# First cross attention of a gated Flamingo block: one half of the heads' softmax moves from VectorE to ScalarE, head by head

## The chip, the core and the metric

The kernel runs on one core of one Trainium2 chip. The metric is the device time of one execution in microseconds (us); the median of three executions of the kernel before is 763.54 us, from 762.81 to 764.01. The engines are named as in the profile: PE is the matmul engine (TensorE; PEld is its weight load), DVE is VectorE, ACT is ScalarE, POOL is GpSimd, SP issues transfers. A row that begins with L451 belongs to line 451 of the kernel before.

## What is computed

Two gated layers stand in a row, each a cross attention and a feed-forward part. The change touches the first cross attention alone:

```python
q = (query @ Wq + bq).reshape(B, SQ, H, HD).transpose(0, 2, 1, 3)       # H = 16 heads, HD = 8
k = (key_value @ Wk + bk).reshape(B, SK, H, HD).transpose(0, 2, 1, 3)   # SK = 77 keys
scores = jnp.einsum('bhqd,bhkd->bhqk', q, k) * scale                    # scale = 8 ** -0.5
scores = jnp.where(key_padding_mask[:, None, None, :], -jnp.inf, scores)
attn = jax.nn.softmax(scores, axis=-1)
attn_out = jnp.einsum('bhqk,bhkd->bhqd', attn, v) ...
attn_out = attn_out @ Wo + bo
```

There are 4 batches of 512 queries, so 16 tiles of 128 queries. For one tile the scores are 16 x 77 = 1232 numbers on each of 128 partitions.

## The kernel before

The program is written out by hand, stage by stage, engine by engine: each engine runs its instructions in the order of its block, and named semaphores hold it where it needs another's result. There is no scheduler. The stage in question runs from about 43 to 147 us of the span and takes one tile `n` in each turn of a loop; the 16 heads are two halves, `h` = 0 and 1, of 616 columns each. PSUM banks 0 and 1 hold the scores of half 0, banks 2 and 3 those of half 1, and there is one copy of each.

What is done for a tile, in the order of its data:

- PE, `score(n, h)` (lines 497 to 508): two small matmuls with the mask (L502) and two with the scores (L506). It may overwrite the banks when `s_used` says that the half of tile n-1 has been read.
- DVE, `top(n, h)` (L444): the maximum of each head. `shifted(n, h)` (L451): the scores less the maximum, from PSUM into the tile `sh` in SBUF; this counts up `s_used`.
- ACT (L570): the exponential of `sh`, one instruction for eight heads, into `pr` (the profile calls it xy, since it lies in that tile). It counts up `exp_done`.
- DVE, `total(m, h)` (L458): the sum of each head's exponentials, into `den`; `inverse(m, h)` (L465): its reciprocal `rd`.
- POOL (L589): probabilities times `rd`; this counts up `pn_done`. Up to tile 9 POOL does a further instruction of preparation for later stages behind each tile.
- PE, `flip(m, b)` (L517): ten transposes of the probabilities in three groups (4, 4 and 2), for the tile two turns back (m = n-2). ACT copies the result from PSUM into `pt` (L560, the first eight; L562, the last two).
- PE (L546): ten products with the values, each as two passes; ACT copies the result with a bias into `attt` (L576); PE projects it one turn later (L531), and DVE adds it to `base` (L474).

The order on each engine in one turn n of the loop: PE runs flip(n-2, 0), the projection of n-3, flip(n-2, 1), flip(n-2, 2), score(n+1, 0), the products of n-2, score(n+1, 1). ACT runs the two copies for n-2, the exponentials of both halves of n, `attt` of n-2. DVE runs top and shifted of (n, 0), the addition of n-3, total(n-1, 0), top(n, 1), inverse(n-1, 0), shifted(n, 1), total(n-1, 1), inverse(n-1, 1).

Of the kernel before, what the change touches and what calls it, by code (L numbers as in the profile page):

```python
# [12 lines left out]
ALU = mybir.AluOpType  # L13
# [3 lines left out]
P = 128  # L17
# [83 lines left out]
def flamingo_kernel(nc, a, out):  # L101
    with ExitStack() as ctx:
        def sb(name, shape, dt=F32, scope=ctx):
            return scope.enter_context(nc.sbuf_tensor(name, shape, dt))
# [70 lines left out]
        @contextmanager  # L175
        def stage(*names):

            with ExitStack() as c:
                sems = [c.enter_context(nc.semaphore(n)) for n in names]
                with nc.Block() as block:  # L180
                    yield block, sems
                nums = [s.num for s in sems]
                nc.all_engine_barrier(sems_to_clear=range(min(nums), max(nums) + 1))
# [44 lines left out]
        with ExitStack() as early:  # L228
# [187 lines left out]


            with ExitStack() as scope:
                sh = sb("sh", [P, 2, WA], scope=scope)
                pr = xy[:, 0:3 * CA * P].rearrange("p (i c) -> p i c", i=3)  # L420
                pt = sb("pt", [P, 2, CA, P], scope=scope)
                qf = [sb(f"qf{i}k", [P, D], scope=scope) for i in range(3)]
                LS, LP, LO = 1, 2, 3

                with stage("v_chain", "d_chain", "p_chain", "pads_done", "s_raw", "s_used", "exp_done", "rd_done", "pn_done",
                           "pt_raw", "pt_lo", "pt_hi", "a_raw", "a_done", "r_raw", "r_done") as (block, sems):
                    (v_chain, d_chain, p_chain, pads_done, s_raw, s_used, exp_done, rd_done, pn_done,
                     pt_raw, pt_lo, pt_hi, a_raw, a_done, r_raw, r_done) = sems
                    WH, HH = WA // 2, HA // 2

                    def scores(h):
                        return banks(2 * h, 2).rearrange("p (b c) -> p b c", c=512)[:, :, 0:G4].rearrange(
                            "p b (h k) -> p b h k", k=SK)
# [4 lines left out]
                    @block.vector  # L438
                    def _(dve):
                        v, d = Chain(dve, v_chain), Chain(dve, d_chain)  # L440

                        def top(n, h):
                            dve.wait_ge(s_raw, 4 * n + 2 * h + 2)
                            v.do(dve.tensor_reduce(mx[:, n % 2, HH * h:HH * (h + 1)].rearrange("p (b h) -> p b h", b=2),  # L444
                                                   scores(h), AX.X, ALU.max))

                        def shifted(n, h):
                            if n >= 2:
                                dve.wait_ge(exp_done, 2 * (n - 2) + h + 1)
                            v.sync()  # L450
                            dve.tensor_tensor(  # L451
                                sh[:, n % 2, WH * h:WH * (h + 1)].rearrange("p (b h k) -> p b h k", b=2, k=SK), scores(h),
                                mx[:, n % 2, HH * h:HH * (h + 1)].rearrange("p (b h) -> p b h", b=2).unsqueeze(3).broadcast_to(
                                    [P, 2, 4, SK]), ALU.subtract).then_inc(s_used, 1)

                        def total(m, h):
                            dve.wait_ge(exp_done, 2 * m + h + 1)
                            d.do(dve.tensor_reduce(den[:, m % 2, HH * h:HH * (h + 1)], probs(m, h), AX.X, ALU.add))  # L458

                        def inverse(m, h):  # L460
                            if m >= 2:
                                dve.wait_ge(pn_done, 2 * (m - 2) + h + 1)
                            d.sync()
                            c = slice(HH * h, HH * (h + 1))
                            dve.reciprocal(rd[:, m % 2, c], den[:, m % 2, c]).then_inc(rd_done, 1)  # L465

                        for n in range(NT + LO):
                            if n < NT:
                                top(n, 0)
                                shifted(n, 0)  # L470
                            if n >= LO:
                                m = n - LO
                                dve.wait_ge(r_raw, m + 1)
                                dve.tensor_tensor(base[:, m, :], bank[7][:, 3 * P:4 * P], base[:, m, :], ALU.add).then_inc(r_done, 1)  # L474
                            if LS <= n < NT + LS:
                                total(n - LS, 0)
                            if n < NT:
                                top(n, 1)
                            if LS <= n < NT + LS:
                                inverse(n - LS, 0)  # L480
                            if n < NT:
                                shifted(n, 1)
                            if LS <= n < NT + LS:
                                total(n - LS, 1)
                                inverse(n - LS, 1)
                            if n == NT:
                                dve.wait_ge(late_in, LATE_IN)
                                v.do(dve.tensor_tensor(sprod[:], fscale[:, 0:1], fscale[:, 1:2], ALU.mult))
                                v.do(dve.reciprocal(rscale[:], fscale))
                                v.sync()  # L490
                                v.do(dve.tensor_scalar(qf[0][:], kern[:], rscale[:, 1:2], None, ALU.mult))
                                v.sync()
                                quantise(dve, v, qf, kern_q[:], D)

                    @block.tensor
                    def _(pe):
                        def score(n, h):
                            u, j = divmod(n, TPB)
                            if n:
                                pe.wait_ge(s_used, 2 * (n - 1) + h + 1)  # L500
                            for g in (2 * h, 2 * h + 1):
                                pe.matmul(bank[g][:, 0:G4], ones_bf[32 * g:32 * g + 1, :],  # L502
                                          mrow_bf[32 * g:32 * g + 1, u:u + 1, :].broadcast_to([1, 4, SK]), start=True, stop=False)
                            for g in (2 * h, 2 * h + 1):
                                rows_g = slice(32 * g, 32 * g + 32)
                                pe.matmul(bank[g][:, 0:G4], qt[rows_g, u, j * P:(j + 1) * P],  # L506
                                          kbd_a[rows_g, u, 4 * g:4 * g + 4, :].rearrange("p h k -> p (h k)"), start=False,
                                          stop=True).then_inc(s_raw, 1)
# [43 lines left out]
                    @block.scalar  # L552
                    def _(act):
                        for n in range(NT + LP):
                            if n >= LP:
                                m = n - LP
                                if m >= 2:
                                    act.wait_ge(a_raw, m - 1)
                                act.wait_ge(pt_raw, 3 * m + 2)
                                act.activation(pt[:, m % 2, 0:8, :].rearrange("p c q -> p (c q)"), banks(4, 2), ACT.Copy).then_inc(pt_lo, 1)  # L560
                                act.wait_ge(pt_raw, 3 * m + 3)
                                act.activation(pt[:, m % 2, 8:10, :].rearrange("p c q -> p (c q)"), bank[6][:, 0:2 * P],  # L562
                                               ACT.Copy).then_inc(pt_hi, 1)
                            if n < NT:
                                for h in range(2):
                                    act.wait_ge(s_used, 2 * n + h + 1)
                                    if n >= 3 and h == 0:
                                        act.wait_ge(pt_raw, 3 * (n - 2))
                                    c = slice(WH * h, WH * (h + 1))
                                    act.activation(pr[:, n % 3, c], sh[:, n % 2, c], ACT.Exp, scale=DA ** -0.5).then_inc(exp_done, 1)  # L570
                            if n >= LP:
                                m = n - LP
                                act.wait_ge(a_raw, m + 1)
                                if m >= 2:
                                    act.wait_ge(r_raw, m - 1)
                                act.activation(attt[:, m % 2, :], bank[7][:, 0:P], ACT.Identity,  # L576
                                               bias=cols_a[:, 2:3]).then_inc(a_done, 1)
# [1093 lines left out]
```

## Time and profile before

| | us |
|---|---|
| median of three executions | 763.54 |
| the profiled execution, its own time | 767.54 |
| its span, first to last instruction | 765.8 |
| of it the stage that changes | about 43 to 147 |
| busy PE / DVE / POOL / ACT, whole span | 592.9 / 503.5 / 418.2 / 345.0 |

The profiled execution is 4.0 us longer than the median of those without a profile. The busy shares above are means over about ten stages with different limits; only this stage bears on the change, and it is read from the engine timelines and the waits of that stretch. In the timeline a row gives the start in us, the duration, engine, line, operation, what it writes and reads, and in brackets the idle time ahead of it with what ended that.

### The profile page before, as it was taken

What the parts mean: (1) busy time and instruction counts of PE and PEld (TensorE: products, weight loads), DVE (VectorE), ACT (ScalarE), POOL (GpSimd) and SP (SyncE); (2) the same over time, 40 slices, a digit from 0 to 9 for tenths busy, and PEclk for the clock granted to TensorE, in tenths of its full rate; (3) what the DMA queues carried; (4) which work ended last, traced back from release to release, by engine and by line L of the source; (5) the groups of instructions that cost most, each with busy time, mean ns of one, the idle gap of its engine ahead of it and who ended that gap; (6) DMA issues with size and microseconds to landing.
All of it is one profiled execution on the core that took longest, in us unless ns stands there. A gap on an engine that the chain in (4) does not pass through costs nothing. (4 is left out here: it accounts for less than half of the span.)

```text
span 765.8 us, 13331 instructions
## 1 busy us (share of the span) xinstructions
PE 592.9 (77%) x4922; PEld 419.2 (55%) x4922; DVE 503.5 (66%) x1117; ACT 345.0 (45%) x603; POOL 418.2 (55%) x345
## 2 busy tenths in 40 slices
PE   5679999595287999997598799999867945768701
PEld 3337777564244677776355367777753623555500
DVE  2766888636558888874543788888636336676496
ACT  2334545271156656654443566566516223343221
POOL 4545673362269999980401999999404015554320
PEclk9558999988689999999899999999998967788755
DMA  8500000000011111110000111111000000000001
GB/s 267 152 1 2 1 1 1 1 1 0 1 28 37 36 30 30 43 23 1 2 1 0 43 35 38 30 30 43 10 1 1 0 1 0 1 0 1 0 1 55
DMA packets 16142, 18.16 MB, mean 24 GB/s; under 512 B 4261, under 2 KB 10831, under 8 KB 16079
## 3 DMA queue, kind: packets, MB, share of 16 engines
q1 hardware_dynamic: 14639, 14.70, 7.5%
q10 hardware_dynamic: 1440, 2.61, 1.0%
q8 instruction: 40, 0.66, 0.4%
q14 instruction: 23, 0.19, 0.1%
HBM read 8.01 MB, written 1.05 MB: 12 GB/s over the span
## 5 line engine op out<-in xcount | busy, mean ns | idle before, releaser
L209 POOL TENSOR_TENSOR rstd<-rstd,minus_half 128x4 f32<-128x4 f32 x32 | 34.0, 1062 | 145.1 <-DVE rstd L203 145.1
L1102 POOL TENSOR_TENSOR rn<-n,minus_half 128x16 f32<-128x16 f32 x32 | 93.7, 2929 | 2.7
L1098 POOL TENSOR_TENSOR qk<-qk 128x512 f32<-128x512 f32 x64 | 80.1, 1273 | 10.8 <-DVE qk L1033 10.8
L1030 DVE TENSOR_TENSOR qk<-ps,rt 128x512 f32<-128x512 f32 x64 | 44.0, 688 | 49.1 <-ACT sq L985 33.4
L1004 ACT ACTIVATE ptb<-ps 128x512 f32<-128x512 f32 x64 | 34.7, 595 | 73.6 <-PE ps L858 73.6
L1107 POOL TENSOR_TENSOR qk<-qk,rn 128x512 f32<-128x512 f32 x64 | 65.4, 1043 | 2.5
L589 POOL TENSOR_TENSOR xy<-xy,rd 128x616 f32<-128x616 f32 x32 | 38.9, 1216 | 42.3 <-DVE rd L465 42.3
L985 ACT ACTIVATE sq<-ps 128x512 f32<-128x512 f32 x64 | 37.6, 598 | 21.9 <-PE ps L821 8.1
L546 PE MATMUL ps<-pt,vbd_a 128*128 128x128 f32 x320 | 41.7, 288 | 6.5 <-ACT pt L560 6.5
L546 PEld LDWEIGHTS ps<-pt,vbd_a 128*128 128x128 f32 x320 | 39.0, 200 | 13.5 <-issue 12.6
L1366 POOL TENSOR_TENSOR sh_c<-gt_c,mx 128x616 f32<-128x616 f32 x16 | 19.9, 1242 | 45.5 <-DVE mx L1328 45.5
L828 PEld LDWEIGHTS ps<-consts,qk 128*128 128x128 f32 x256 | 29.2, 140 | 27.4 <-issue 15.6
L1033 DVE TENSOR_TENSOR qk<-ps,rt 128x512 f32<-128x512 f32 x64 | 43.6, 681 | 0.0
L1240 DVE SCALAR_TENSOR_TENSOR qk<-ps,cols_b,pb 128x512 f32<-128x512 f32 (+1 forms) x24 | 17.8, 749 | 37.6 <-PE ps L1137 27.7
L1067 DVE TENSOR_REDUCE mx<-ps 128x8 f32<-128x1024 f32 x32 | 39.0, 1218 | 4.4 <-PE ps L852 4.4
L828 PE MATMUL ps<-consts,qk 128*128 128x128 f32 x256 | 35.3, 276 | 7.8 <-POOL qk L1107 5.4
L1071 DVE TENSOR_TENSOR pb<-ps,mx 128x1024 f32<-128x1024 f32 x32 | 39.2, 1225 | 3.0
L865 PE MATMUL ps<-vv,ptb 128*64 128x65 f32 x512 | 36.5, 224 | 4.6 <-DVE xy L1056 4.6
L893 PE MATMUL ps<-wo_b,ont 128*128 128x128 f32 x256 | 34.6, 278 | 7.0 <-ACT ont L1011 7.0
L1060 DVE TENSOR_REDUCE n<-sq 128x16 f32<-128x1024 f32 x32 | 38.7, 1209 | 0.0
L978 ACT ACTIVATE qkt<-ps 128x512 f32<-128x512 f32 x64 | 35.5, 598 | 6.8 <-PE ps L828 6.8
L850 PE MATMUL ps<-qkt 64*64 64x128 f32 x512 | 36.0, 280 | 2.8 <-ACT qkt L978 2.8
(200 smaller groups left out, 1634.6 us busy)
## 6 DMA issues: line engine op xcount, KB each, us to landing
vv<-vv SPq DMA_DIRECT2D x62, 130.0 KB, 2.3
wqkv<-in_wqkv SPq DMA_DIRECT2D x1, 1536.0 KB, 16.5
x<-in_x SPq DMA_DIRECT2D x4, 256.0 KB, 8.7
out<-xy SPq DMA_DIRECT2D x4, 256.0 KB, 2.3
w_b<-in_w_b SPq DMA_DIRECT2D x1, 682.0 KB
tmat<-in_tmat SPq DMA_DIRECT2D x1, 616.0 KB, 7.7
w<-in_w ACTq DMA_DIRECT2D x1, 512.0 KB, 4.1
rot<-in_c_rot ACTq DMA_DIRECT2D x1, 512.0 KB, 8.3
```

The costliest lines, as they stand in the source:

```text
L546: mm = pe.matmul(bank[7][:, 0:P], vbd_a[:, c, m // TPB, :], pt[:, m % 2, c, :], start=(c == 0), stop=(c == CA - 1))
L589: pool.tensor_tensor(probs(m, h), probs(m, h), rd[:, m % 2, HH * h:HH * (h + 1)].unsqueeze(2).broadcast_to([P, HH, SK]), ALU.mult).then_in ...
L828: t = pe.transpose(dst[:, c * P:(c + 1) * P], qk[:, m % 3, kind, c * P:(c + 1) * P], ident)
L985: act.activation(sq[:, kind, :], src, ACT.Square).then_inc(done, 1)
L1030: dve.tensor_tensor(qk[:, n % 3, kind].rearrange("p (h d) -> p h d", d=DH), src.rearrange("p (h d) -> p h d", d=DH), rt[:, layer, j, i:i + ...
L1033: return dve.tensor_tensor(qk2[:, kind].rearrange("p (h a e) -> p h a e", a=2, e=DH // 2), src.rearrange("p (h a e) -> p h a e", a=2, e=DH ...
L1060: dve.tensor_reduce(n2[:, n % 2, :], sq[:].rearrange("p k (h d) -> p (k h) d", d=DH), AX.X, ALU.add).then_inc(n2_done, 1)
L1067: v.do(dve.tensor_reduce(mx[:, k, 0:HB], s8, AX.X, ALU.max))
L1071: dve.tensor_tensor(pb[:, k], s8, mx[:, k, 0:HB].unsqueeze(2).broadcast_to([P, HB, P]), ALU.subtract).then_inc(s_used, 1)
L1098: pool.tensor_tensor(w, w, qk2[:, kind], ALU.add).then_inc(done, 1)
L1102: pool.tensor_tensor(rn[:, k, :], n2[:, k, :], minus_half[:], ALU.pow).then_inc(rn_done, 1)
L1107: pool.tensor_tensor(w, w, rn[:, k, HB * kind:HB * (kind + 1)].unsqueeze(2).broadcast_to([P, HB, DH]), ALU.mult).then_inc(done, 1)
```

## The change

For half 1 (heads 8 to 15) of each of the 16 tiles, DVE no longer subtracts the maximum and no longer sums the exponentials. It computes `neg`, the maximum times -8 ** -0.5, in one instruction of 8 columns, and ACT takes the exponentials straight from the score banks, one instruction for each head, with `neg` as the bias of each partition and the sum of the exponentials as a second output into `den`. Half 0 is left as it was. `sh` shrinks to one half. The banks of half 1 are now given back to PE by `exp_done` (ACT's last head) instead of `s_used`. The reciprocal of half 1 waits for ACT's heads instead of for DVE's own sum.

```diff
+                        def negated(n):
+                            if n >= 2:
+                                dve.wait_ge(exp_done, 2 * (n - 1))
+                            v.sync()
+                            dve.tensor_scalar(neg[:, n % 2, :], mx[:, n % 2, HH:HA], -DA ** -0.5, None,
+                                              ALU.mult).then_inc(neg_done, 1)
...
+                            if h:
+                                dve.wait_ge(exp_done, 2 * m + 2)
                             d.sync()
...
                             if n < NT:
-                                shifted(n, 1)
+                                negated(n)
                             if LS <= n < NT + LS:
-                                total(n - LS, 1)
                                 inverse(n - LS, 1)
...
                             if n:
-                                pe.wait_ge(s_used, 2 * (n - 1) + h + 1)
+                                pe.wait_ge(exp_done, 2 * n) if h else pe.wait_ge(s_used, n)
...
-                                for h in range(2):
-                                    act.wait_ge(s_used, 2 * n + h + 1)
-                                    if n >= 3 and h == 0:
-                                        act.wait_ge(pt_raw, 3 * (n - 2))
-                                    c = slice(WH * h, WH * (h + 1))
-                                    act.activation(pr[:, n % 3, c], sh[:, n % 2, c], ACT.Exp, scale=DA ** -0.5).then_inc(exp_done, 1)
+                                act.wait_ge(s_used, n + 1)
+                                if n >= 3:
+                                    act.wait_ge(pt_raw, 3 * (n - 2))
+                                act.activation(pr[:, n % 3, 0:WH], sh[:, n % 2, :], ACT.Exp, scale=DA ** -0.5).then_inc(exp_done, 1)
+                                act.wait_ge(neg_done, n + 1)
+                                if n >= 2:
+                                    act.wait_ge(rd_done, 2 * (n - 1))
+                                for i in range(HH):
+                                    ins = act.activation(probs(n, 1)[:, i, :], bank[2 + i // 4][:, SK * (i % 4):SK * (i % 4 + 1)], ACT.Exp,
+                                                         bias=neg[:, n % 2, i:i + 1], scale=DA ** -0.5,
+                                                         accum_out=den[:, n % 2, HH + i:HH + i + 1])
+                                ins.then_inc(exp_done, 1)
```

ACT in the middle of the stage, one turn of the loop before (pt are the two copies, xy the exponentials, attt the result of the products; the names in brackets are the semaphores waited for):

```order
L560 ACTIVATE pt<-ps 128x1024 [waits pt_raw,a_raw]
L562 ACTIVATE pt<-ps 128x256 [waits pt_raw]
L570 ACTIVATE xy<-sh 128x616 [waits pt_raw,s_used]
L570 ACTIVATE xy<-sh 128x616 [waits s_used]
L576 ACTIVATE attt<-ps,cols 128x128 [waits r_raw,a_raw]
```

and the same turn now:

```order
L569 ACTIVATE pt<-ps 128x1024 [waits pt_raw,a_raw]
L571 ACTIVATE pt<-ps 128x256 [waits pt_raw]
L577 ACTIVATE xy<-sh 128x616 [waits pt_raw,s_used]
L582 ACTIVATE xy,den<-ps,neg 128x77 [waits rd_done,neg_done]
L582 ACTIVATE xy,den<-ps,neg 128x77 x7
L591 ACTIVATE attt<-ps,cols 128x128 [waits r_raw,a_raw]
```

The second exponential of a turn became eight instructions of 77 columns, which stand behind the copies of `pt` and the first exponential and ahead of `attt`.

PE in the middle of the stage before, from the products to the next turn's first transposes (pt is what ACT copied, kbd_a and qt make the scores):

```order
L546 MATMUL ps<-pt,vbd_a 128x128 [waits pt_lo,r_done,a_done]
L546 MATMUL ps<-pt,vbd_a 128x128 x7
L546 MATMUL ps<-pt,vbd_a 128x128 [waits pt_hi]
L546 MATMUL ps<-pt,vbd_a 128x128
L502 MATMUL ps<-mrow_bf,ones_bf 128x308 [waits s_used]
L502 MATMUL ps<-mrow_bf,ones_bf 128x308
L506 MATMUL ps<-kbd_a,qt 128x308 x2
L517 MATMUL ps<-consts,xy 128x128 [waits pt_lo,pn_done]
```

and now:

```order
L555 MATMUL ps<-pt,vbd_a 128x128 [waits pt_lo,r_done,a_done]
L555 MATMUL ps<-pt,vbd_a 128x128 x7
L555 MATMUL ps<-pt,vbd_a 128x128 [waits pt_hi]
L555 MATMUL ps<-pt,vbd_a 128x128
L511 MATMUL ps<-mrow_bf,ones_bf 128x308 [waits exp_done]
L511 MATMUL ps<-mrow_bf,ones_bf 128x308
L515 MATMUL ps<-kbd_a,qt 128x308 x2
L526 MATMUL ps<-consts,xy 128x128 [waits pt_lo,pn_done]
```

PE's order is the same; the scores of half 1 wait for ACT's `exp_done` where they waited for DVE's `s_used`, and the next turn's transposes stand behind them.

## Rows read from the trace of the kernel before

**Rows 1.** Busy time by stretch; columns PE, PEld, DVE, ACT, POOL, granted clock, DMA:

```profile
43.00:60.00 17.00, 14.19 (x67) 8.52 (x64) 14.00 (x22) 5.37 (x8) 9.44 (x11) 0.50 0.00 1
60.00:131.00 71.00, 67.63 (x541) 53.01 (x540) 59.34 (x108) 36.19 (x61) 41.05 (x32) 0.99 0.01 1
```

**Rows 2.** Who waited for whom, 60 to 131 us; total, times, longest:

```profile
PE ps L546 <- ACT pt L560: 3.4, 12, 0.3
```

**Rows 3.** Timeline of one turn of the loop, all engines:

```profile
72.79 0.31 PE L502 MATMUL ps<-mrow_bf,ones_bf 1*128 1x308 bf16 x2
...
73.56 0.66 PE L517 MATMUL ps<-consts,xy 128*128 128x128 f32 x4
...
74.47 0.29 DVE L474 TENSOR_TENSOR base<-ps,base 128x128 f32<-128x128 f32 x1 [0.57 <-PE ps L531]
...
74.97 1.02 ACT L560 ACTIVATE pt<-ps 128x1024 f32<-128x1024 f32 x1 [1.70 <-PE ps L517]
...
76.09 0.19 DVE L465 RECIPROCAL rd<-den 128x8 f32<-128x8 f32 x1
...
76.14 2.47 PE L546 MATMUL ps<-pt,vbd_a 128*128 128x128 f32 x20 [0.28 <-ACT pt L560]
76.15 0.72 ACT L570 ACTIVATE xy<-sh 128x616 f32<-128x616 f32 x1
76.27 0.80 DVE L451 TENSOR_TENSOR sh<-ps,mx 128x616 f32<-128x616 f32 x1
...
76.99 0.78 DVE L458 TENSOR_REDUCE den<-xy 128x8 f32<-128x616 f32 x1
...
78.54 0.31 PE L502 MATMUL ps<-mrow_bf,ones_bf 1*128 1x308 bf16 x2
```

**Rows 4.** ACT's instructions by line and shape; busy us, mean ns, idle before:

```profile
L560 ACT ACTIVATE pt<-ps 128x1024 f32<-128x1024 f32 x16 | 16.4, 1023 | 27.1 <-PE ps L517 27.1
...
L562 ACT ACTIVATE pt<-ps 128x256 f32<-128x256 f32 x16 | 6.1, 379 | 0.0
L576 ACT ACTIVATE attt<-ps,cols 128x128 f32<-128x128 f32 x16 | 5.9, 367 | 19.2 <-PE ps L546 19.2
...
L1473 ACT ACTIVATE attt<-ps 128x128 f32<-128x128 f32 x16 | 4.4, 277 | 31.4 <-PE ps L1432 31.4
...
L304 ACT ACTIVATE tg<-vecs 128x4 f32<-128x4 f32 x1 | 0.2, 196 | 0.0
```

**Rows 5.** Timeline, four ACT instructions with a bias pointer back to back, and one:

```profile
158.39 2.42 ACT L754 ACTIVATE hidt<-ps,cols 128x512 f32<-128x512 f32 x4
...
168.59 0.69 ACT L754 ACTIVATE hidt<-ps,cols 128x512 f32<-128x512 f32 x1
```

**Rows 6.** DVE's nearest small instruction by line and shape:

```profile
L203 DVE TENSOR_SCALAR rstd<-mv 128x4 f32<-128x4 f32 x32 | 5.4, 170 | 1.1
```

**Rows 7.** Timeline of the stage's first turns:

```profile
45.92 0.79 DVE L444 TENSOR_REDUCE mx<-ps 128x8 f32<-128x616 f32 x1
...
47.60 0.44 PE L502 MATMUL ps<-mrow_bf,ones_bf 1*128 1x308 bf16 x2
...
47.83 1.23 PE L506 MATMUL ps<-kbd_a,qt 32*128 32x308 f32 x4
...
51.53 0.43 PE L502 MATMUL ps<-mrow_bf,ones_bf 1*128 1x308 bf16 x2 [0.78 <-DVE sh L451]
...
52.93 2.39 PE L517 MATMUL ps<-consts,xy 128*128 128x128 f32 x10
```

**Rows 8.** Timeline of the stage's end and of the second cross attention:

```profile
133.56 0.72 ACT L570 ACTIVATE xy<-sh 128x616 f32<-128x616 f32 x1
...
136.05 0.37 ACT L576 ACTIVATE attt<-ps,cols 128x128 f32<-128x128 f32 x1 [0.82 <-PE ps L546]
...
138.76 2.47 PE L546 MATMUL ps<-pt,vbd_a 128*128 128x128 f32 x20 [1.05 <-ACT pt L560]
...
713.54 2.47 PE L1432 MATMUL ps<-pt_c,vbd_c 128*128 128x128 f32 x10 [1.15 <-DVE x L1334]
```

More of the change, by code:

```diff
@@ L418, in flamingo_kernel @@
             with ExitStack() as scope:
-                sh = sb("sh", [P, 2, WA], scope=scope)
+                sh = sb("sh", [P, 2, WA // 2], scope=scope)
+                neg = sb("neg", [P, 2, HA // 2], scope=scope)
                 pr = xy[:, 0:3 * CA * P].rearrange("p (i c) -> p i c", i=3)
@@ L423, in flamingo_kernel @@
                 LS, LP, LO = 1, 2, 3
-                with stage("v_chain", "d_chain", "p_chain", "pads_done", "s_raw", "s_used", "exp_done", "rd_done", "pn_done",
+                with stage("v_chain", "d_chain", "p_chain", "pads_done", "s_raw", "s_used", "neg_done", "exp_done", "rd_done", "pn_done",
                            "pt_raw", "pt_lo", "pt_hi", "a_raw", "a_done", "r_raw", "r_done") as (block, sems):
-                    (v_chain, d_chain, p_chain, pads_done, s_raw, s_used, exp_done, rd_done, pn_done,
+                    (v_chain, d_chain, p_chain, pads_done, s_raw, s_used, neg_done, exp_done, rd_done, pn_done,
                      pt_raw, pt_lo, pt_hi, a_raw, a_done, r_raw, r_done) = sems
@@ L451, in shifted @@
                             dve.tensor_tensor(
-                                sh[:, n % 2, WH * h:WH * (h + 1)].rearrange("p (b h k) -> p b h k", b=2, k=SK), scores(h),
+                                sh[:, n % 2, :].rearrange("p (b h k) -> p b h k", b=2, k=SK), scores(h),
                                 mx[:, n % 2, HH * h:HH * (h + 1)].rearrange("p (b h) -> p b h", b=2).unsqueeze(3).broadcast_to(
                                     [P, 2, 4, SK]), ALU.subtract).then_inc(s_used, 1)
+                        def negated(n):
[4 more added lines that the diff above has]
+                                              ALU.mult).then_inc(neg_done, 1)
                         def total(m, h):
```

## The prediction

> **What bounds the kernel now.** I read the busy times by stretch first, to see whose stage this is. From 60 to 131 us PE is busy 67.6 of 71 us at a granted clock of 0.99, DVE 59.3, POOL 41.1, ACT 36.2 [rows 1]. So PE sets the pace, and ACT has most time to spare. Then the waits of that stretch: PE's one wait for another engine is the products' wait for ACT's copy of the transposes, 3.4 us in 12 turns, 0.28 in a turn [rows 2, 3]; ACT waits 1.7 us in each turn for the transposes [rows 3]. Last the timeline of one turn, from the scores of half 1 at 72.79 to the next ones at 78.54 [rows 3]: a period of 5.75 us, of which PE works 5.47. DVE is not what PE waits for: it stands idle 0.57 us in a turn, for the projection. What the change takes from DVE is therefore taken from an engine that waits anyway.
>
> **What leaves.** DVE loses L451 and L458 of half 1, 0.80 + 0.78 us in a turn, and gets `negated`, 8 columns: the nearest row, a tensor-scalar of 4 columns, takes 0.17 [rows 6]. I cost this at nothing gained, since PE waits for none of it. ACT loses one exponential of 616 columns, 0.72 us.
>
> **What comes: the price of a head.** Eight instructions of 77 columns take its place. ACT's slope is (1023 - 379) / 768 = 0.839 ns per column; a bias pointer adds 367 - 277 = 90 ns [rows 4]. From L576 (128 columns with a pointer, out of PSUM) a head's duration is 367 - 51 x 0.839 = 324 ns. Back to back, four of L754 take 2.42 us and one 0.69, so they start (2.42 - 0.69) / 3 = 0.577 apart: an overlap of 0.11 [rows 5]. A head without its sum then costs 0.324 - 0.11 = 0.214 from start to start. No row has the sum as a second output. Its bounds are zero, if it comes with the pass, and the smallest ACT instruction, 0.196 [rows 4], with none of it overlapped; overlapped like the others that would be 0.09. I take 0.12, nearer to the overlapped end because all of ACT's neighbours overlap, with something lost because the sum is complete only behind the last element. That makes s = 0.334 from start to start and 0.444 for the last head. Eight heads run 7 x 0.334 + 0.444 = 2.78 us.
>
> The Trainium skill, ScalarE: Activation LUTs, section What ACT_TABLE_LOAD costs, gives about 280 ns plus 0.833 ns per column for an ACTIVATE with a pointer bias and an overlap of 93 ns, and no price for the sum: by it 251 ns from start to start, and an estimate of 772 us by the sum below. The trace's L754 disagrees a little: the page would give 0.613 us from start to start, the row 0.577 [rows 5].
>
> **Where it lies.** The heads are not beside PE's work but in a new ring with it. The score banks of half 1 exist once and are now given back by ACT's last head. ACT reaches the heads only behind the copies of `pt`, which wait for the turn's transposes, and on PE those stand behind the scores of half 1. So: scores of half 1, transposes, copies, first exponential, eight heads, scores of half 1 again. From rows 3: scores to copy 74.97 - 72.79 = 2.18; copy to first exponential 76.15 - 74.97 = 1.18; the first head starts 0.72 - 0.11 = 0.61 behind that; heads 2.78; the hand-over to PE 0.12 (the copy ends at 75.99, the products start at 76.14, and their weights some hundredths earlier). Together 6.87 us against 5.75: 1.12 us more in a turn. PE's products still fit beside the copies and exponentials, and PE stands idle 1.12 us ahead of the scores of half 1. That wait holds everything queued behind it on PE: the transposes, the projection, the next scores.
>
> Is something else later than ACT? `neg` must be there when the first head could start, 3.97 us behind the scores. DVE's reciprocal stands at 76.09 and its next at 76.27, 3.48 behind; with 0.17 `neg` is ready at 3.65. It is hidden by 0.3 us; a longer chain on DVE would cost its excess. The second reciprocal of a turn no longer waits for L451 and L458, so POOL's second half comes earlier than before and is no limit. `attt` now queues behind the heads, but PE needs it only 1 us behind the scores that the heads release: hidden.
>
> **The sum.** The full ring runs in turns 2 to 14, 13 times: 13 x 1.12 = 14.6. At the start there are no copies yet, but the ring of scores, maximum, `neg` and heads is exposed twice [rows 7]. The first maximum of half 1 ends at 46.71, `neg` at 46.91, heads run 46.95 to 49.73, scores at 49.85 instead of 47.60. They take 1.46 at the half clock of 0.50 granted there [rows 1, 7], to 51.31; the maximum and the reciprocal take 0.87 to the start of `neg`, heads run 52.38 to 55.16, scores of tile 2 at 55.28 instead of 51.53: 3.75 us. In the last turn the first exponential starts at 133.56, so the heads run from 134.17 to 136.95, and `attt` ends at 137.21 instead of 136.42 [rows 8]: 0.8. The sum is 14.6 + 3.75 + 0.8 = 19.2 us. The profiled execution would go from 767.54 to 786.7; it lies 4.0 above the median, and I take that to stay, so the median goes to 782.7.
>
> **Rivals.**
> (1) The clock falls. In the forecast PE has a gap of 1.12 us in each turn. In this stage's end gaps of 1.05 leave the products at 2.47 us for 20, full speed; in the second cross attention a gap of 1.15, among shorter ones, was followed by products at 2.47 us for 10, half speed [rows 8]. The forecast lies between. At half clock the ring's PE part is dearer: scores 1.46 against 0.77, and ten transposes 2.39, where from their start to the copy it is now 1.41 with the projection in it [rows 3, 7]; about 1.6 us for one turn. Every second turn: 6.5 x 1.6 = 10 more, 793; every turn: 803. For it speaks the gap's size; against it that PE is still busy 80% of a turn in one long piece.
> (2) The sum is dear: 0.196 on top, s = 0.41, heads 3.39 us. The ring is 7.48, and 13 x 1.73 + 5.0 + 1.4 = 28.9, so 792. If nothing overlaps at all, s = 0.52 and the heads run 4.16: the ring is 8.25, and 32.5 + 6.5 + 2.2 = 41, so 805.
> (3) The sum is free: s = 0.214, heads 1.82, the ring 5.91. Then 13 x 0.16 + 1.8 = 3.9, so 767.5.
> (4) No slower: ACT takes small instructions faster than its large ones say. L304 has 4 columns in 196 ns; with 73 columns more it is 257, and with 0.11 overlapped and the pointer and the sum hidden, s is 0.147 [rows 4, 5]. The ring is then 5.38, below PE's 5.75, and PE keeps its pace; the start costs 0.8: 764.3. It decides from s = 0.19 downwards, where the ring passes 5.75. Against it stand L576 and L754, both with the pointer's cost on show. Faster it hardly gets, for PE's own 5.47 of work and its 0.28 for the copy stay.
>
> **How the numbers follow.** Forecast, with the clock held and s from 0.25 to 0.38 (some 770 to 789): 0.50. Clock falling in a good part of the turns: 0.20. Dear sum: 0.16. Free sum: 0.09. No slower: 0.05. The range 768 to 803 leaves out the cheap end of the free sum and the fourth rival (about 0.08) and the ends of the first two (about 0.09). A difference of 0.2%, 1.5 us, is about what can be told from no change: slower 0.95, same 0.03, faster 0.02.
>
> **What would show it.** Right: a row of 128 heads of 77 columns near 0.44 us each, about 0.33 from start to start; PE's scores of half 1 waiting for ACT by some 1.1 us a turn; a period near 6.9 us; ACT busy some 2 us more in a turn; DVE with some 2 us idle; granted clock near 1 behind 62 us. Wrong: a separate long instruction for the sums, heads that wait for `neg`, a clock that drops in mid-stage, or PE still waiting only for the copy. The steps I hold for weakest are the price of the sum and the clock.

## The result, and the profile after

The changed kernel takes 777.94 us (median of four executions, 772.87 to 781.41) against 763.77 for the kernel before in the same comparison: 1.018 times, with a 95% interval from 1.014 to 1.022. It is 14.2 us slower; 19.2 were forecast. A second comparison, further below, gives 1.020.

The profiled execution of the changed kernel happens to be the quickest of the four (772.87 us, span 770.8), and its first stage of all ends 4.2 us earlier than in the profile before. So the stage is compared by its own length, from the first score matmul to the last addition to `base`. These are the instructions of those two lines, before and after; the columns are duration in ns (least, median, greatest) and the start of the first and the last in us:

```profile
L502 PE MATMUL ps<-mrow_bf,ones_bf x64: 301/306/435, 42.8 to 130.2; 1*128 1x308 bf16 x64
...
L474 DVE TENSOR_TENSOR base<-ps,base x16: 284/292/294, 63.0 to 147.3; 128x128 f32<-128x128 f32 x16
```

```profile
L511 PE MATMUL ps<-mrow_bf,ones_bf x64: 301/306/437, 38.6 to 138.8; 1*128 1x308 bf16 x64
...
L484 DVE TENSOR_TENSOR base<-ps,base x16: 291/291/294, 61.6 to 158.1; 128x128 f32<-128x128 f32 x16
```

From 42.8 to 147.3 is 104.5 us; from 38.6 to 158.1 is 119.5. The stage is 15.0 us longer. The span is only 5.0 us longer (770.8 against 765.8), since 4.2 us ahead of the stage and 5.8 us behind it went the other way, in parts of the program that are the same in both.

Busy time by stretch after (columns as in [rows 1]) shows what changed place:

```profile
43.00:60.00 17.00, 11.25 (x58) 7.99 (x58) 8.40 (x16) 9.78 (x52) 7.13 (x6) 0.51 0.00 0
60.00:131.00 71.00, 60.19 (x482) 46.82 (x482) 39.65 (x88) 49.65 (x213) 37.54 (x30) 1.00 0.01 1
```

Against [rows 1], DVE fell from 59.3 to 39.7 us, ACT rose from 36.2 to 49.7, and PE, which set the pace, fell from 67.6 to 60.2: it now waits. (Part of these falls is that the stretch now holds 10.8 turns of 6.58 us where it held 12.3 of 5.75.) The granted clock is 1.00 where it was 0.99. No engine is full; what grew is a wait. The waits from 62 to 128 us name it:

```profile
PE ps L511 <- ACT xy L582: 7.7, 10, 0.8
...
PE ps L555 <- ACT pt L569: 2.8, 10, 0.3
```

The wait for the copies is the one of before, 0.28 us in a turn [rows 2]. The wait of the scores for ACT's heads is new, 0.77 us in each of ten turns. One turn in the timeline, the rows that answer to [rows 3]:

```profile
66.44 0.31 PE L511 MATMUL ps<-mrow_bf,ones_bf 1*128 1x308 bf16 x2 [0.78 <-ACT xy L582]
...
66.59 0.68 PE L515 MATMUL ps<-kbd_a,qt 32*128 32x308 f32 x4
...
68.61 1.02 ACT L569 ACTIVATE pt<-ps 128x1024 f32<-128x1024 f32 x1 [1.97 <-PE ps L526]
...
69.78 2.47 PE L555 MATMUL ps<-pt,vbd_a 128*128 128x128 f32 x20 [0.28 <-ACT pt L569]
69.80 0.72 ACT L577 ACTIVATE xy<-sh 128x616 f32<-128x616 f32 x1
69.92 0.17 DVE L461 TENSOR_SCALAR neg<-mx 128x8 f32<-128x8 f32 x1
...
70.41 0.33 ACT L582 ACTIVATE xy<-ps,neg 128x77 f32<-128x77 f32 x1
70.61 0.21 ACT L582 ACTIVATION_READ_ACCUMULATOR xy<-ps,neg 128x1 f32 x1
70.70 0.34 ACT L582 ACTIVATE xy<-ps,neg 128x77 f32<-128x77 f32 x1
...
72.71 0.26 ACT L582 ACTIVATION_READ_ACCUMULATOR xy<-ps,neg 128x1 f32 x1
72.80 0.43 ACT L591 ACTIVATE attt<-ps,cols 128x128 f32<-128x128 f32 x1
...
73.03 0.31 PE L511 MATMUL ps<-mrow_bf,ones_bf 1*128 1x308 bf16 x2 [0.77 <-ACT xy L582]
```

This is the ring, read down the rows: scores at 66.44, copies at 68.61 (2.17 behind), first exponential at 69.80 (1.19), first head at 70.41 (0.61), end of the last head's sum at 72.97 (2.56), scores again at 73.03 (0.06). A turn is 6.59 us where it was 5.75 [rows 3]. `neg` is ready at 70.09, 0.32 us ahead of the first head. Each head turned out to be two instructions, an ACTIVATE and, 0.20 us behind its start, a read of the accumulator (the row with READ_ACCUMULATOR); 0.09 us behind the start of that, the next head starts.

### The profile page after: what moved, and what is told of

Its sections match the earlier page's. It is cut to its first block and busy times, and to the rows that moved or that the text cites. A ratio compares the mean times of both kernels' runs of the same rounds, so it can differ in the third digit from the quotient of the medians.

```text
span 770.8 us, 13571 instructions
## 1 busy us (share of the span) xinstructions
PE 583.6 (76%) x4922; PEld 412.8 (54%) x4922; DVE 482.5 (63%) x1101; ACT 371.8 (48%) x843; POOL 417.5 (54%) x345
## 5 line engine op out<-in xcount | busy, mean ns | idle before, releaser
L582 ACT ACTIVATE xy<-ps,neg 128x77 f32<-128x77 f32 x128 | 39.5, 349 | 2.2 <-DVE neg L461 2.2
```

What stands on the lines that cost most here:

```text
L582: ins = act.activation(probs(n, 1)[:, i, :], bank[2 + i // 4][:, SK * (i % 4):SK * (i % 4 + 1)], ACT.Exp, bias=neg[:, n % 2, i:i + 1], sca ...
```

## Experiments

Each time is a median with the kernel before measured beside it. The ratio, with its 95% interval in brackets, is worked out from the single executions; it is not the quotient of the two medians and differs from it by up to 0.3%. Because the rest of the program varies from run to run (last section), the steady turn, between starts of the copies of `pt` in the middle of the stage, and the length of the stage are given for each as well. The changed kernel's are 6.58 and 119.5 us, those of the kernel before 5.74 to 5.75 and 104.5.

The theory is the ring: the score banks of half 1 exist once, ACT's last head gives them back, and by PE's order the copies ahead of the heads stand behind those very scores. The rivals are that ACT's added work costs what it costs wherever it stands (queue), that PE's clock pays for its gaps (clock), and that DVE's relief or the sums are what counts.

### The sums back on DVE

```diff
-                            if h:
-                                dve.wait_ge(exp_done, 2 * m + 2)
...
                                 negated(n)
                             if LS <= n < NT + LS:
+                                total(n - LS, 1)
                                 inverse(n - LS, 1)
...
-                                                         bias=neg[:, n % 2, i:i + 1], scale=DA ** -0.5,
-                                                         accum_out=den[:, n % 2, HH + i:HH + i + 1])
+                                                         bias=neg[:, n % 2, i:i + 1], scale=DA ** -0.5)
```

> The changed kernel with one part undone: the heads stay with ACT, but without the sum as a second output; DVE sums half 1 again as before the change. Ring theory (score banks of half 1, transposes, copies, first exponential, heads, banks again): the eight accumulator reads vanish, heads start 0.21 to 0.25 us apart instead of 0.30, the turn is 5.95 to 6.2 us instead of 6.58, and the whole is 767 to 772 us, some 6 to 9 under the changed kernel. If the accumulator reads only filled time in which each head waits for its own end, heads stay 0.30 apart, the turn stays 6.58 and the time stays near 778. If it is DVE's relief that matters in the changed kernel, this one is slower than it, over 778, since DVE gets 0.78 us a turn back.

Measured: 765.17 us against 762.35, 1.002 times (0.999 to 1.005); the turn is 5.86 and the stage 107.1 us. Its timeline in the middle of the stage (the second row is the last of the first row's eight, by itself):

```profile
96.25 1.84 ACT L581 ACTIVATE xy<-ps,neg 128x77 f32<-128x77 f32 x8
...
97.71 0.39 ACT L581 ACTIVATE xy<-ps,neg 128x77 f32<-128x77 f32 x1
...
98.15 0.30 PE L510 MATMUL ps<-mrow_bf,ones_bf 1*128 1x308 bf16 x2
```

The granted clock is 1.00 there as in the changed kernel. Eight heads run in 1.84 us. The first starts at 96.25 and the last at 97.71, so they start 0.208 us apart, close to what was worked out ahead (0.214). The read of the accumulator therefore costs 0.092 us a head. Seven steps of it, and a last head that ends 0.08 us sooner, make the heads 2.56 - 1.84 = 0.72 us shorter, and the turn is 6.58 - 5.86 = 0.72 us shorter, though DVE got 0.78 us of work back. In this order every hundredth of ACT's heads is in the turn, and DVE's work is not. Turn and time came out below the expected 5.95 to 6.2 and 767 to 772, since I had allowed for heads as far as 0.25 apart.

### Four heads more

```diff
...
+                                for i in range(4):
+                                    act.activation(more[:, i, :], bank[2][:, SK * i:SK * (i + 1)], ACT.Exp,
+                                                   bias=neg[:, n % 2, i:i + 1], scale=DA ** -0.5, accum_out=mden[:, i:i + 1])
                                 for i in range(HH):
                                     ins = act.activation(probs(n, 1)[:, i, :], ...
```

> The changed kernel with four more heads in each turn: the first four of half 1 are exponentiated once more, with bias and sum, into tiles that nobody reads. It does more work than is asked. Ring theory: 4 x 0.30 = 1.2 us more in each of 12 turns and about 1.2 more in each of two turns of the start and one of the end, so the turn is 7.78 us and the time 794 to 797 us while the granted clock stays near 1; PE's wait ahead of the scores grows from 0.78 to 1.98 us. Clock theory: with that gap the clock falls to half in a good part of the turns, the turn is 8.5 us or more in these, and the time passes 800. If ACT has spare time for the heads, as its busy share says, the time stays under 785.

Measured: 798.6 us against 762.35, 1.046 times (1.041 to 1.052); stage 142.4 us. Its turns are 7.80 to 7.82 us in four cases and 7.89 to 8.55 in the other eight, 8.07 in the mean. PE in the middle of the stage:

```profile
79.11 0.31 PE L513 MATMUL ps<-mrow_bf,ones_bf 1*128 1x308 bf16 x2 [2.00 <-ACT xy L587]
...
83.09 4.64 PE L557 MATMUL ps<-pt,vbd_a 128*128 128x128 f32 x20
87.66 0.32 PE L513 MATMUL ps<-mrow_bf,ones_bf 1*128 1x308 bf16 x2
...
91.02 2.47 PE L557 MATMUL ps<-pt,vbd_a 128*128 128x128 f32 x20 [0.29 <-ACT pt L571]
95.48 0.31 PE L513 MATMUL ps<-mrow_bf,ones_bf 1*128 1x308 bf16 x2 [2.00 <-ACT xy L587]
```

Both theories hold here, each for its share. An undisturbed turn, 87.66 to 95.48, is 7.82 us, 1.24 more than 6.58 for four heads of 0.30: the ring. Behind a gap of 2.0 us the clock can fall, and the products then take 4.64 us instead of 2.47; such a turn, 79.11 to 87.66, is 8.55. Four of the twelve groups of products are slow in this way; one fall touches up to two of the spans between copies, so eight of those are longer. Over twelve turns the clock adds (8.07 - 7.81) x 12, some 3 us; the four heads add 1.23 x 12, some 15, by the ring. The median lies between the two expectations, above the 794 to 797 of the ring alone and below the 800 of the clock theory.

### The wait alone

```diff
-                                pe.wait_ge(s_used, 2 * (n - 1) + h + 1)
+                                pe.wait_ge(exp_done, 2 * n) if h else pe.wait_ge(s_used, 2 * n - 1)
```

This is made in the kernel before.

> The kernel before with only the wait changed: the score banks of half 1 are given back by ACT's one exponential of 616 columns (0.72 us) instead of by DVE's subtraction. Ring theory: the ring with 0.72 in place of 2.56 us of heads is about 4.9 us in a turn, under PE's 5.75, so the steady turn stays 5.75; the start loses 0.7 to 1.5 us in two turns; 763.5 to 766 us. If a wait for ACT ahead of the scores costs by itself, whatever its length, the turn gets longer than 5.9 and the time passes 767.

Measured: 764.75 us against 762.35, 1.002 times (0.998 to 1.005); the turn is 5.75 and the stage 104.4 us. So it is not the wait for ACT that costs, but the length of what stands in the ring.

### The scores later

In the changed kernel the scores of half 1 move on PE from the end of a turn to behind the next turn's transposes.

```diff
                         score(0, 0)
-                        score(0, 1)
...
                                 flip(n - LP, 1)
                                 flip(n - LP, 2)
+                            if n < NT:
+                                score(n, 1)
                             if n + 1 < NT:
                                 score(n + 1, 0)
...
-                            if n + 1 < NT:
-                                score(n + 1, 1)
```

> The changed kernel with PE's order changed at one place: the scores of half 1 of a tile are computed a turn later, behind that turn's ten transposes, instead of ahead of them. The work of every engine is the same. Ring theory: the ring is opened, since the copies no longer stand behind ACT's heads by way of PE; the turn falls from 6.58 to 5.5 to 5.9 us (PE then waits some 0.5 us for attt ahead of the projection) and the time to 762 to 768 us. Queue theory (ACT's 2 us more of work in a turn cost what they cost wherever they stand): the turn stays above 6.4 and the time above 775.

Measured: 765.55 us against 762.35, 1.004 times (1.002 to 1.007); the turn is 5.97 and the stage 107.0 us. With the same instructions on every engine 11.3 to 12.4 us of the stage went away (against the changed kernel's two profiles): the queue theory falls. The scores of the two halves, now side by side, also take PE less time (last section); but PE was waiting in the changed kernel, and the same edit gained nothing in the kernel before (control below). The turn is a little above the 5.5 to 5.9 expected, because the wait for `attt` ahead of the projection is longer than I had put it. PE:

```profile
97.28 0.49 PE L539 MATMUL ps<-w,attt 128*128 128x128 f32 x2 [0.87 <-ACT attt L590]
97.61 0.82 PE L526 MATMUL ps<-consts,xy 128*128 128x128 f32 x6
98.36 0.33 PE L511 MATMUL ps<-mrow_bf,ones_bf 1*128 1x308 bf16 x4
98.50 0.70 PE L515 MATMUL ps<-kbd_a,qt 32*128 32x308 f32 x8
```

A second ring has taken over: heads, `attt`, projection, the remaining transposes, scores, maximum, heads. The first ring could also be opened on ACT, with the heads ahead of the copies; that was not run.

### Opening the second ring

Two more changes of order, each on top of the one before. First, in the kernel with the scores later, the projection goes behind the transposes on PE:

```diff
-                            if n >= LO:
-                                m = n - LO
-                                pe.wait_ge(a_done, m + 1)
-                                ...
                             if LP <= n < NT + LP:
                                 flip(n - LP, 1)
                                 flip(n - LP, 2)
+                            if n >= LO:
+                                m = n - LO
+                                pe.wait_ge(a_done, m + 1)
+                                ...
```

> The changed kernel with the scores of half 1 behind the transposes, and the projection behind them as well, so that the transposes do not wait for attt, which ACT gives out behind its heads. Ring theory: the ring left in the run before (heads, attt, projection, transposes, scores, maximum, heads; 5.97 us) loses the transposes, 0.75 us, but the addition that waits for the projection stands ahead of the maximum on DVE: a turn of 5.4 to 5.6 us, stage about 100 us, time 757 to 762 us. If ACT's queue itself is the limit (some 4.9 us of work), the turn is 5.0 to 5.2; if the heads cost what they cost wherever they stand, it stays at 5.97 or above.

Measured: 753.14 us against 763.43, 0.987 times (0.981 to 0.993); the turn is 5.47 and the stage 99.9 us, as expected of the ring; the time is a little below what was expected.

Then, on top of that, the addition to `base` goes behind the sum and the reciprocal of half 0 on DVE:

```diff
                                 shifted(n, 0)
+                            if LS <= n < NT + LS:
+                                total(n - LS, 0)
+                                inverse(n - LS, 0)
                             if n >= LO:
                                 ...  # the addition to base
-                            if LS <= n < NT + LS:
-                                total(n - LS, 0)
                             if n < NT:
                                 top(n, 1)
-                            if LS <= n < NT + LS:
-                                inverse(n - LS, 0)
-                            if n < NT:
                                 negated(n)
```

> As the kernel with scores and projection later, and on DVE the addition to base stands behind the sum and reciprocal of half 0 instead of ahead of them. Ring theory: maximum and heads no longer wait for the projection by way of DVE; what is left is heads, attt, projection, scores, maximum, neg, heads: 0.2 + 0.85 + 0.8 + 0.35 + 2.56 + 0.4 and hand-overs, a turn of 5.1 to 5.3 us, and 753 to 759 us, under both kernels. If nothing of that ring binds, the turn is as in the run without this edit.

Measured: 749.62 us against 763.43, 0.982 times (0.977 to 0.987); the turn is 5.31 and the stage 95.9 us. Faster than both kernels, with the heads and their sums on ACT.

### Controls: is it the order or the work taken from DVE?

The edit of the scores alone, in the kernel before:

> The control for the run with the scores later: the same one change of PE's order made in the kernel before, whose half 1 still goes through DVE. In that run the scores of both halves, standing together on PE, took 0.85 us instead of two times 0.83, so PE's work in a turn falls from 5.47 to about 4.75. Ring theory: the kernel before has no ring over ACT to open; what it gains is what PE gives up, until DVE (about 5.2 us of work in a turn) or the copies are the limit: a turn of 5.3 to 5.6 us against 5.75, and 757 to 762 us. If PE was not the limit of the kernel before, the turn stays 5.75 and the time 763.

Measured: 761.76 us against 763.43, 1.000 times (0.996 to 1.003); the turn is 5.77 and the stage 105.9 us. The median lies just inside the expected 757 to 762, but the ratio shows no gain, and the turn was missed: PE's work fell from 53.2 to 48.7 us between 62 and 118 us, and the turn did not fall with it. The waits of that stretch say why:

```profile
ACT xy L569 <- DVE sh L451: 7.1, 9, 0.8
...
DVE mx L444 <- PE ps L506: 6.0, 10, 0.6
PE ps L517 <- POOL xy L588: 4.4, 10, 0.5
```

The scores of half 1 now stand behind the transposes, and DVE waits for them, 0.6 us in a turn. So DVE comes to the subtraction and the sum of half 1 later, its reciprocal follows them, POOL's second half later still, and PE waits for POOL ahead of the last six transposes. The pace had only changed hands.

The whole order, in the kernel before: PE's as in the changed kernel's fastest run, and on DVE, as the edit shows, all sums and reciprocals of the last tile ahead of the addition:

```diff
                                 shifted(n, 0)
+                            if LS <= n < NT + LS:
+                                total(n - LS, 0)
+                                inverse(n - LS, 0)
+                                total(n - LS, 1)
+                                inverse(n - LS, 1)
                             if n >= LO:
                                 ...  # the addition to base
-                            if LS <= n < NT + LS:
-                                total(n - LS, 0)
                             if n < NT:
                                 top(n, 1)
-                            if LS <= n < NT + LS:
-                                inverse(n - LS, 0)
-                            if n < NT:
                                 shifted(n, 1)
-                            if LS <= n < NT + LS:
-                                total(n - LS, 1)
-                                inverse(n - LS, 1)
```

> The control for the fastest order: the kernel before (half 1 through DVE, no heads on ACT) with PE's order of that run (transposes, projection, scores of both halves, products) and on DVE all sums and reciprocals of the last tile ahead of the addition and the second maximum. It tells whether that order alone gives the gain or needs the work taken from DVE. If DVE's relief matters once the ring is open: DVE has about 4.95 us of work in a turn and stands still some 0.5 for the scores, so the turn is 5.4 to 5.6 us and the time 754 to 758, above the 749.6 of the changed kernel in that order. If the order alone does it: 5.1 to 5.3 us and 747 to 751.

Measured: 749.06 us against 762.38, 0.986 times (0.978 to 0.994); the turn is 5.34 to 5.35 and the stage 95.4 us. That is as fast as the changed kernel in its best order. The turn lies just above the 5.1 to 5.3 expected if the order alone gives the gain, the time within its 747 to 751. So that reading is the right one: in the orders that were run, the order alone gives the gain, and the work taken from DVE gives nothing on top of it. The two kernels do not stop at the same limit, though. Waits from 62 to 118 us, first this control, then the changed kernel in its best order:

```profile
PE ps L544 <- DVE base L479: 8.6, 11, 0.8
```

```profile
PE ps L540 <- ACT attt L588: 5.2, 10, 0.6
```

In the control DVE is busy 51.7 of these 56 us and PE waits for it. In the changed kernel DVE is busy 39.5, and PE waits for ACT's `attt`, which stands behind the heads. DVE's relief is there, but the heads on ACT bring a limit of nearly the same size.

The changed kernel in its best order, with the sums on DVE:

> As the kernel with all three changes of order, but the sums of half 1 are left with DVE, as in the run without the second output. Heads 1.84 us in a turn instead of 2.56, DVE 0.78 us more. Ring theory: the ring loses 0.7 us and falls under PE's work and its wait for the copies, about 5.0 us; the turn is 4.95 to 5.15 and the time 751 to 756 us. If ACT's order no longer matters at this point and DVE's work does, it is no faster than the run with the sums on ACT.

Measured: 755.63 us against 763.43, 0.988 times (0.983 to 0.994); the turn is 5.36 to 5.37, twice 5.81 to 5.82, and the stage 98.9 us. The expected 4.95 to 5.15 was missed. ACT's ring got shorter, but the waits show the limit elsewhere:

```profile
ACT pt L565 <- PE ps L523: 10.8, 11, 1.0
...
PE ps L523 <- POOL xy L599: 6.9, 11, 1.0
```

Half 1's reciprocal waits for DVE's sum again, POOL for it, and PE for POOL. In the two longer turns POOL's further instruction lasts 2.36 us instead of 1.27. Here the sum of half 1 stands late in DVE's turn, behind the second maximum; ahead of the addition, as in the control above, it was not run in the changed kernel.

### The changed kernel once more

> The changed kernel once more, on the chip and with the runs of the kernel before that the control has. Its first profile has one turn at half clock near the end of the stage, and the spread of its runs is wide. Ring theory: the steady turn is 6.58 us again, the stage 117.5 to 120 us, according to whether a half-clock turn is in it, and the time 1.6 to 2.1% over the kernel before. If the clock makes the difference and not the ring, the turn differs by more than 0.1 us between the two profiles.

Measured: 778.82 us against 762.38, 1.020 times (1.014 to 1.026). The turn is 6.58 to 6.59 again, the stage 118.3 us, this time with no half-clock turn at its end. The pace of the turn does not depend on the clock's luck.

## Why the prediction was right

**Who sets the pace, and that DVE's relief is worth nothing.** Right for the kernel as it stood. DVE lost 0.80 + 0.78 us in a turn and got 0.17, and the turn got no shorter for it; giving DVE 0.78 us a turn back (the sums on DVE) cost nothing. It holds for this order: once the order is changed, DVE nearly sets the pace of the kernel before (the control of the whole order).

**The ring.** Right in every link: 2.17, 1.19, 0.61, 2.56, 0.06 against 2.18, 1.18, 0.61, 2.78, 0.12. Opening it by order alone took 11.3 to 12.4 us off the stage; four more heads lengthened it by 1.24 us a turn; a short occupant (0.72 us) left it harmless.

**The price of a head.** Mechanism right, size a little high. Without its sum a head starts every 0.208 us (0.214 worked out). The sum is an instruction of its own that overlaps like all the others and costs 0.092, the 0.09 that stood as the overlapped price. I took 0.12, and 0.334 instead of 0.300 made the heads 2.78 us instead of 2.56. A separate long instruction for the sums stood among the signs of being wrong: a separate one there is, 0.23 us by itself, but most of it is overlapped, so it is not dear. The row of heads is 0.35 us each, not 0.44, since the read is counted apart. By the Trainium skill's figures (ScalarE: Activation LUTs, What ACT_TABLE_LOAD costs) heads without sums would, by estimate, start 0.251 apart; this trace's 0.208 disagrees.

**The sum.** The turn grew by 0.83 us and not 1.12: 0.22 of the difference is the heads, 0.06 the hand-over to PE, which I took from a copy and its products and which is shorter here. And the full ring bound in 12 turns, not 13: in the first of them PE is still at half clock and is itself the limit (its products take 4.35 us), so that turn lost nothing. The three terms against the two profiles of the changed kernel, all from starts of scores and additions:

| | forecast | first profile | second profile |
|---|---|---|---|
| start, to the scores of half 1 of tile 2 | +3.75 | +3.2 | +3.2 |
| the turns | +14.6 | +9.6 | +10.1 |
| the end | +0.8 | +2.1 | +0.5 |
| sum | 19.2 | 15.0 | 13.8 |

At the start the same heads and hand-over stand twice, 2 x (0.22 + 0.06) = 0.56 us, which is the difference there. The heads, the hand-over and the number of turns were all put too high, so none of these errors made up for another. The stage's growth of 13.8 to 15.0 us and the measured 14.2 and 16.4 agree within the spread of the runs.

**The rivals.** The clock: it held. The granted clock is 1.00 from 60 to 131 us with a gap of 0.77 in each turn. Behind that it fell once within the stage, at its end in the first profile, for one run of products:

```profile
145.67 0.49 PE L540 MATMUL ps<-w,attt 128*128 128x128 f32 x2 [0.59 <-ACT attt L591]
145.99 0.82 PE L526 MATMUL ps<-consts,xy 128*128 128x128 f32 x6
147.86 4.10 PE L555 MATMUL ps<-pt,vbd_a 128*128 128x128 f32 x20 [1.05 <-ACT pt L569]
```

4.10 us instead of 2.47 is the 1.6 us by which the two profiles differ at the end. With gaps of 2.0 the clock does fall in the middle of the stage (four heads more), so this rival was real, but not at this size. The dear sum did not come true, and the free sum is what the run without sums shows: a turn of 5.86, where 5.91 was forecast for that case. The fourth rival, heads at 0.19 or less, did not come true either.

## What to carry to other kernels

A buffer's release belongs to the cost of an instruction that reads it: work moved to an engine with time to spare is still dear if the only copy of a PSUM bank is held until that engine, late in its own queue, has read it. Follow such a release round to the buffer's next writer and back, and add up the ring; if it passes the turn, change the order of the engine in the ring before moving work. Here two moves in the order of PE and a new order on DVE gave 1.4% without the heads on ACT and 1.8% with them, alike within their intervals.

## What the runs showed of the hardware

The sum as a second output of an ACTIVATE is a separate instruction on ACT. Its two rows in the changed kernel, by shape:

```profile
L582 ACT ACTIVATE xy<-ps,neg 128x77 f32<-128x77 f32 x128 | 39.5, 349 | 2.2 <-DVE neg L461 2.2
...
L582 ACT ACTIVATION_READ_ACCUMULATOR xy<-ps,neg 128x1 f32 x128 | 29.8, 233 | 0.0
```

It lasts 0.23 us and costs 0.092 between neighbours. The two rows overlap, so the sum of their busy times, 69 us, is not time on ACT: 128 heads at 0.30 are 38.

Score matmuls of the two halves that stand together on PE nearly double up. Each half uses two groups of 32 rows; where the halves were apart, four matmuls took 0.68 us, and where they stood together eight took 0.70 (the rows of the scores later, above, against those of the turn). That takes work from PE, but by itself it gained nothing in the kernel before (the edit of the scores alone); how much of the gain of the whole order is due to it was not measured.

The rest of the program behind the stage, alike in all these kernels, took 612 to 615 us in seven of the profiles and 618 to 620 in five. The second cross attention makes the difference. These are its products in the profile before, one of the five, and after, one of the seven (columns as in the first rows of the result):

```profile
L1432 PE MATMUL ps<-pt_c,vbd_c x160: 274/275/552, 644.4 to 725.9; 128*128 128x128 f32 x160
```

```profile
L1447 PE MATMUL ps<-pt_c,vbd_c x160: 273/275/422, 655.9 to 730.9; 128*128 128x128 f32 x160
```

From the first to the last they take 81.5 us before and 75.0 after, at a granted clock of 0.81 and 0.90; it is 81.4 to 81.5 us in all five and 74.9 to 75.3 in all seven. That is most of the spread between the profiles behind the stage, and the reason why the stage's length was read and not only the time; what decides it in a run stays open.
